# A two-layer vision tower: rotary partners by a shuffle, candidate lists merged by products, and a centring step without its own division

## The reference

```
h = tokens of 28x28 patches, class token, times a position table
h = layernorm(h + attention0(h))    # 8 heads of 16, rotary q and k, heads mixed before and after softmax
h = layernorm(h + ffn0(h))          # 16 experts; each takes its top 8 tokens of every image, results scatter-added
h = layernorm(h + attention1(h))    # causal attention blended with a moving average
h = layernorm(h + ffn1(h))          # 8 Sinkhorn rounds on 4160x8 gates; each expert takes its top 8 tokens of all
```

## Time and profile before

| | |
|---|---|
| time, median of 3 runs | 761.0 us (759.26 to 763.16) |
| the profiled execution | 762.83 us, span 761.0 us |
| granted TensorE clock, mean | 0.894 |
| PE busy | 587.0 us (77%) |
| DVE busy | 488.3 us (64%) |
| ACT busy | 336.0 us (44%) |
| POOL busy | 247.3 us (32%) |

### The profile page before, as it was taken

The page is one execution under the profiler, slowest core; times in us unless marked ns, Lnnn a source line. Parts: engine busy times, 40 slices in busy tenths (PEclk is TensorE's granted clock), DMA queues, the critical chain, the costliest instruction groups (busy, mean ns, idle before and its releaser), DMA issues. The chain is left out here.

```text
span 761.0 us, 20823 instructions
## 1 busy us (share of the span) xinstructions
PE 587.0 (77%) x8519; PEld 485.0 (64%) x8519; DVE 488.3 (64%) x880; ACT 336.0 (44%) x871; POOL 247.3 (32%) x251
## 2 busy tenths in 40 slices
PE   1999999999999999776179887766799999960002
PEld 1788888888888888664074476656677777740002
DVE  3175665666666666654536489955688888827852
ACT  0022444443444444453145356530578788846500
POOL 5344333333333333300104024432345555420001
PEclk9999999999999999987589999968699999965555
DMA  9364322222333379100430392000000000002200
GB/s 369 147 219 162 124 102 107 90 109 109 127 127 127 127 185 147 23 3 1 157 73 1 43 132 50 2 1 2 2 3 1 0 0 1 4 1 72 68 1 4
DMA packets 36813, 57.51 MB, mean 76 GB/s; under 512 B 20360, under 2 KB 33784, under 8 KB 34200
## 3 DMA queue, kind: packets, MB, share of 16 engines
q1 hardware_dynamic: 36666, 56.72, 26.4%
q0 software_dynamic: 96, 0.07, 0.0%
HBM read 50.24 MB, written 6.55 MB: 75 GB/s over the span
## 5 line engine op out<-in xcount | busy, mean ns | idle before, releaser
L387 PE MATMUL a_bank<-a_x,a_tok_w 128*128 128x256 f32 (+1 forms) x608 | 150.5, 390 | 16.0 <-DVE a_ht L640 16.0
L387 PEld LDWEIGHTS a_bank<-a_x,a_tok_w 128*128 128x128 f32 (+1 forms) x608 | 113.1, 192 | 37.6 <-issue 21.3
L129 POOL TENSOR_TENSOR a_qt<-a_qp,data 128x512 f32<-128x512 f32 x64 | 71.9, 1153 | 2.1 <-POOL a_qp L751 1.6
L751 POOL TENSOR_TENSOR a_qp<-a_rope 128x260 f32<-128x260 f32 x16 | 11.7, 734 | 168.9 <-DVE a_rope L575 168.9
L287 ACT ACTIVATE a_at<-a_bank 65x256 f32<-65x256 f32 x128 | 38.9, 390 | 25.0 <-PE a_bank L264 25.0
L569 DVE SCALAR_TENSOR_TENSOR a_ht<-a_bank,data 128x256 f32<-128x256 f32 x16 | 7.7, 484 | 64.6 <-PE a_bank L387 64.6
L1182 POOL TENSOR_TENSOR base<-h_tok,bias 65x512 f32<-65x512 f32 x16 | 29.8, 1866 | 55.2 <-ACT h_tok L1165 55.2
L1562 POOL TENSOR_TENSOR b_e<-b_e,b_inv 128x585 f32<-128x585 f32 (+1 forms) x32 | 35.4, 1109 | 23.7 <-DVE b_inv L1412 23.7
L264 PE MATMUL a_bank<-a_mix,a_e 64*65 64x64 f32 x1024 | 38.6, 227 | 2.2 <-ACT a_at L287 2.2
L200 ACT ACTIVATE a_e<-a_e 128x390 f32<-128x390 f32 (+1 forms) x48 | 24.1, 510 | 32.1 <-DVE a_e L180 32.0
L264 PEld LDWEIGHTS a_bank<-a_mix,a_e 64*65 64x65 f32 x1024 | 34.2, 140 | 6.0 <-issue 3.9
(11 more groups left out here) (255 smaller groups left out, 1452.5 us busy)
## 6 DMA issues: line engine op xcount, KB each, us to landing
a_x<-in_x SPq DMA_DIRECT2D x16, 2304.0 KB, 7.8
lag_rows<-a_kernel SPq DMA_DIRECT2D x1, 4192.5 KB, 38.3
lags<-lag_rows SPq DMA_DIRECT2D x1, 2112.5 KB
out<-e_plain SPq DMA_DIRECT2D x16, 130.0 KB
expert_weights<-in_w SPq DMA_DIRECT2D x2, 1024.0 KB, 6.0
lags<-lag_rows SPq DMA_DIRECT2D x1, 2047.5 KB
base<-places SPq DMA_DIRECT2D x1, 1560.0 KB
a_tok_w<-in_tok_w SPq DMA_DIRECT2D x1, 1152.0 KB, 6.8
```

What stands on the lines that cost most here:

```text
L129: nc.gpsimd.tensor_tensor(qt[:, b * BLOCKS * P:(b + 1) * BLOCKS * P].rearrange("p (c h i) -> p c h i", i=qb, h=HEADS), wide(by_image[:, b, ...
L387: mm = nc.tensor.matmul(banks[0][:, 0:GP], w[0:rows, k * DIM:(k + 1) * DIM], x[p][0:rows, k * GP:(k + 1) * GP], start=(k == 0), stop=(k == ...
```

## The change

It has three parts.

1. Rotary in `embed_and_attend`. The products with `wqs` and `wks` and their tables go. One query and one key product follow each other, into banks 6 and 7, and keys no longer wait for the rotated queries. DVE multiplies each by the cosine and by the sine table (whose rows are now swapped), and one `stream_shuffle` of the query's and the key's sine halves (128x520) swaps partitions i and i^4. `EMBED` moves fillers. `scale` now stands ahead of `normalise` in DVE's loop.
2. `scatter_and_norm`: the multiplication by 1/128 goes; the subtraction becomes one `scalar_tensor_tensor` that takes the sums with the factor -1/128 and adds.
3. `norm_and_route`: the four DRAM writes and reads of the lists and the chosen tokens go. The lists are spread by a masked product on DVE (`by_list`), then by a matrix product with a 0/1 table into 64 rows of 128; the choice is made on 64 partitions; the 64x64 table comes from a product with ones. Three small tables are added to the input, four 128-column weight blocks and two columns are removed.

```diff
-EMBED = (0, 4, 5, 11, 15, KT + 1)
+EMBED = (0, 3, 6, 11, 15, KT + 1)
...
                 wait_past(pe, S.tok_saved, g - 3)
-                product(6, D("wq"), h)
-                product(7, D("wqs"), h).then_inc(S.q_done, 1)
-
-            def keys(g, h):
-
-                pe.wait_ge(S.rope_a, 2 * g + 2)
-                product(6, D("wk"), h)
-                product(7, D("wks"), h).then_inc(S.k_done, 1)
+                product(6, D("wq"), h).then_inc(S.q_done, 1)
+                product(7, D("wk"), h).then_inc(S.k_done, 1)
...
-                rotate(0, 6, "bq", cos4, S.rope_a)
-                rotate(1, 7, "bqs", sin4, S.rope_a)
+                rotate(sine[:, 0, :], 6, "bq", sin4).then_inc(S.rope_ka, 1)
+                rotate(cosine[:, 0, :], 6, "bq", cos4).then_inc(S.rope_a, 1)
 
             def rotate_keys(g):
                 dve.wait_ge(S.k_done, g + 1)
-                rotate(2, 6, "bk", cos4, S.rope_ka)
-                rotate(3, 7, "bks", sin4, S.rope_ka)
-                dve.wait_ge(S.rope_ka, 2 * g + 2)
-                nc.vector.tensor_tensor(kt[:, :].rearrange("p (b t) -> p b t", b=GI), rope[2][:, :, :],
-                                        rope[3][:, :, :], ALU.add).then_inc(S.kt_ready, 1)
+                rotate(sine[:, 1, :], 7, "bk", sin4).then_inc(S.rope_ka, 1)
+                dve.wait_ge(S.rope_ka, 3 * g + 2)
+                rotate(cosine[:, 1, :], 7, "bk", cos4).then_inc(S.rope_ka, 1)
+                nc.vector.stream_shuffle(swapped[:, :, :], sine[:, :, :], [i ^ 4 for i in range(32)]).then_inc(S.rope_swapped, 1)
+                dve.wait_ge(S.rope_ka, 3 * g + 3)
+                dve.wait_ge(S.rope_swapped, g + 1)
+                nc.vector.tensor_tensor(kt[:, :], cosine[:, 1, :], swapped[:, 1, :], ALU.add).then_inc(S.kt_ready, 1)
...
                     values(g + 1, 1 - p)
+                if exists(g - 1):
+                    scale(g - 1)
+                if exists(g + 1):
                     normalise(nc, dve, g + 1, e[1 - p], total, inv, S)
                 if exists(g - 1):
-                    scale(g - 1)
                     save_logits(g - 1)
...
-                pool.wait_ge(S.rope_a, 2 * g + 2)
-                nc.gpsimd.tensor_tensor(qp[:, :].rearrange("p (b t) -> p b t", b=GI), rope[0][:, :, :],
-                                        rope[1][:, :, :], ALU.add).then_inc(S.q_sum, 1)
+                pool.wait_ge(S.rope_a, g + 1)
+                pool.wait_ge(S.rope_swapped, g + 1)
+                nc.gpsimd.tensor_tensor(qp[:, :], cosine[:, 0, :], swapped[:, 0, :], ALU.add).then_inc(S.q_sum, 1)
...
                 nc.vector.tensor_reduce(total[n % 3][:, :], summed, AX.X, ALU.add).then_inc(S.summed, 1)
                 dve.wait_ge(S.summed, n + 1)
-                nc.vector.tensor_scalar(mean[n % 3][:, :], total[n % 3][:, :], 1.0 / DIM, None,
-                                        ALU.mult).then_inc(S.mean_ready, 1)
-                dve.wait_ge(S.mean_ready, n + 1)
...
-                nc.vector.tensor_tensor(zc[n % 3][:, :, :], summed, wide(mean[n % 3][:, :].unsqueeze(2), [TOKENS, GI, DIM]),
-                                        ALU.subtract).then_inc(S.centred, 1)
+                nc.vector.scalar_tensor_tensor(out=zc[n % 3][:, :, :], in0=wide(total[n % 3][:, :].unsqueeze(2), [TOKENS, GI, DIM]),
+                                               scalar=-1.0 / DIM, in1=summed, op0=ALU.mult, op1=ALU.add).then_inc(S.centred, 1)
...
+            def in_lists(n, a):
+                nc.vector.tensor_tensor(by_list[:, n, :, :], wide(T("list_of").unsqueeze(2), [P, LISTS, TOP]),
+                                        wide(a[:, :].unsqueeze(1), [P, LISTS, TOP]), ALU.mult).then_inc(S.listing, 1)
...
             then(nc.vector.max(best[:, :], cand[:, :]))
+            in_lists(0, best)
             then(nc.vector.max_index(place[:, :], best[:, :], cand[:, :]))
             then(nc.vector.tensor_copy(placef[:, :], place[:, :]))
-            nc.vector.tensor_scalar(placef[:, :], placef[:, :], T("block_base"), None, ALU.add).then_inc(S.listed, 1)
-
-            dve.wait_ge(S.lists, 32)
-            then(nc.vector.max(top[:, :], lv[:, :]))
-            then(nc.vector.max_index(pos[:, :], top[:, :], lv[:, :]))
+            then(nc.vector.tensor_scalar(placef[:, :], placef[:, :], T("block_base"), None, ALU.add))
+            in_lists(1, placef)
+
+            dve.wait_ge(S.lists, 1)
+            then(nc.vector.tensor_copy(lists[:, :], banks[2][0:SL, 0:P]))
+            then(nc.vector.max(top[:, :], lists[:, :]))
+            then(nc.vector.max_index(pos[:, :], top[:, :], lists[:, :]))
             then(nc.vector.tensor_copy(posf[:, :], pos[:, :]))
-            then(nc.vector.tensor_tensor(hit[:, :, :], wide(T("iota", E).unsqueeze(1), [E, TOP, P]),
-                                         wide(posf[:, :].unsqueeze(2), [E, TOP, P]), ALU.is_equal))
-            then(nc.vector.tensor_tensor(hit[:, :, :], hit[:, :, :], wide(ln[:, :].unsqueeze(1), [E, TOP, P]), ALU.mult))
-            nc.vector.tensor_reduce(chosen[:, 0, :], hit[:, :, :], AX.X, ALU.add).then_inc(S.chosen, 1)
-            nc.vector.tensor_scalar(chosen[:, 1, :], top[:, :], 0.5, None, ALU.is_gt).then_inc(S.chosen, 1)
-
-            dve.wait_ge(S.slots, 48)
+            then(nc.vector.tensor_tensor(posf[:, :], posf[:, :], T("slot_of", SL), ALU.mult))
+            then(nc.vector.tensor_reduce(at[:, :], posf[:, :], AX.X, ALU.add))
+            dve.wait_ge(S.lists, 2)
+            then(nc.vector.scalar_tensor_tensor(out=hit[:, :], in0=T("iota", SL), scalar=at[:, :], in1=banks[3][0:SL, 0:P],
+                                                op0=ALU.is_equal, op1=ALU.mult))
+            then(nc.vector.tensor_reduce(mine[:, 0:1], hit[:, :], AX.X, ALU.add))
             nc.vector.tensor_copy(take[:, :], mine[:, 0:1]).then_inc(S.index, 1)
-            then(nc.vector.tensor_scalar(same[:, :], everyone[:, :], mine[:, 0:1], None, ALU.is_equal))
+            nc.vector.tensor_scalar(alone[:, :], T("ident", SL)[:, 0:SL], mine[:, 0:1], None, ALU.mult).then_inc(S.chosen, 1)
...
+            dve.wait_ge(S.everyone, 1)
+            then(nc.vector.tensor_scalar(same[:, :], banks[4][0:SL, 0:SL], mine[:, 0:1], None, ALU.is_equal))
...
+            for n in range(2):
+                pe.wait_ge(S.listing, n + 1)
+                nc.tensor.matmul(banks[2 + n][0:SL, 0:P], T("slots_of_expert"),
+                                 by_list[:, n, :, :].rearrange("p l k -> p (l k)"), start=True, stop=True).then_inc(S.lists, 1)
+            pe.wait_ge(S.chosen, 1)
+            nc.tensor.matmul(banks[4][0:SL, 0:SL], T("ones", SL)[:, 0:SL], alone[:, :], start=True,
+                             stop=True).then_inc(S.everyone, 1)
```

More of the change, by code:

```diff
@@ L326, in embed_and_attend @@
         ht = [sb(f"ht{i}", [P, GI, TOKENS]) for i in range(2)]
-        rope = [sb(f"rope{i}", [P, GI, TOKENS]) for i in range(4)]
+        cosine, sine, swapped = (sb(n, [P, 2, GT]) for n in ("cosine", "sine", "swapped"))
         qp, kt = sb("qp", [P, GT]), sb("kt", [P, GT])
@@ L828, in route_and_gather @@
         banks = [ctx.enter_context(nc.psum_tensor(f"r_bank{i}", [P, 512], F32)) for i in range(8)]
-        S = named_semaphores(R.ctx, nc, "r_", "step shifted exp_done probs turned best saved loaded loaded_rest read ident_done "
+        S = named_semaphores(R.ctx, nc, "r_", "step shifted exp_done probs turned best saved loaded loaded_rest read "
                   "picked gathered stored adapt bv_spread value_bias padded")
@@ L1044, in scatter_and_norm @@
         zc = [sb(f"zc{i}", [TOKENS, GI, DIM]) for i in range(3)]
[L1045 to L1046 removed]
+        total, var, sd, rs = ([sb(f"{n}{i}", [TOKENS, GI]) for i in range(3)]
+                                          for n in ("total", "var", "sd", "rs"))
         T = lambda name, rows=P: R.tables[0:rows, TABLES[name][0]:TABLES[name][0] + TABLES[name][1]]
@@ L1598, in norm_and_route @@
         banks = [ctx.enter_context(nc.psum_tensor(f"e_bank{i}", [P, 512], F32)) for i in range(6)]
-        S = named_semaphores(R.ctx, nc, "e_", "step col_sum col_done turned listed saved lists chosen chosen_saved slots index "
+        S = named_semaphores(R.ctx, nc, "e_", "step col_sum col_done turned listed listing lists chosen everyone index "
                   "got turned2 x_ready y_done y_ready turned3 gated mixed squared root scattered weights "
```

68 lines of the change are left out of this document (25 added, 43 removed).

## The result

| | before | after |
|---|---|---|
| time, median of 4 runs each | 761.11 us (759.26 to 763.16) | 718.26 us (717.28 to 718.97) |
| ratio, 95% interval | | 0.9435 (0.9408 to 0.9463) |
| span of the profiled execution | 761.0 us | 716.8 us |
| granted TensorE clock, mean | 0.894 | 0.900 |

A forecast was written before the change was run, and what follows sets the result against it. PE's order bounds `embed_and_attend`, DVE `scatter_and_norm`, and one chain of DVE steps and DMA round trips the final selection. Gains of 19.6 + 12.9 + 10.2 = 42.7 us take 761.0 to 718 us; 8 in 10 between 712 and 727.

The forecast's parts named there:

- 0.88 + 0.53: `embed_and_attend`, per period: two products fewer on PE save 0.88 us, the vanished wait for `a_hw` ahead of the tail 0.53.
- 18.6 us named as a sign: `embed_and_attend`: a period of 18.6 us would show the forecast right.
- forecast 11.9 to 13.0: `embed_and_attend`: with scores at 108.78, `a_hw` ends by 120.7, or by 121.8 if held up by a whole POOL piece.
- 15 x 0.88: `embed_and_attend`: removed products save 0.88 us in 15 of 16 groups, 13.2 us; the last iteration with keys counts nothing.
- 19.6 us: `embed_and_attend`: whole gain of part 1, 13.2 us from products and 6.4 from the wait in 12 periods.
- PE's clock: Rival: where the clock rises and falls between stages may shift, 3 us either way; larger loss or several shortfalls, chance 0.04.
- Forecast 12.9: `scatter_and_norm`: eleven intervals shrink from 4.20 to 3.2 us, 11.0, plus 1.9 in the drain; ends 9.6 and 14.2.
- a long loop: `scatter_and_norm`: loop from scatter over sums, subtraction and ACT to the scatter two groups on, 6.15 us for two intervals.
- Forecast 10.2: `norm_and_route`: best candidates to `e_take` falls from 14.4 to 4.2 us, products hidden; fetch still ends last, 0.5 us cover.
- The wait for `a_hw`: Rival in `embed_and_attend`: PE still waits 0.5 us every period, 6.4 us less gain, 724.5 us; chance 0.11.
- The new centring: Rival in `scatter_and_norm`: it waits for POOL as the multiplication did, part 2 gives next to nothing, 731 us; chance 0.06.
- The 1.9: Slower rival, `embed_and_attend`: shuffle time above 1.9 us is waiting in 12 to 13 periods; 5.2 eats all; chance 0.02.

The follow-up runs named there:

- part1: The kernel before with the rotary part alone (with `EMBED` and DVE's new order): 746.36 us, ratio 0.9797.
- part3: The kernel before with only the lists merged by products in `norm_and_route`: 751.25 us, ratio 0.9863.
- part2: The kernel before with the new centring of `scatter_and_norm` alone: 747.62 us, ratio 0.9805.
- sums_in_psum: The kernel before with the sums in PSUM instead of SBUF, the multiplication by 1/128 kept: 749.59 us, ratio 0.9821.
- after_again: The changed kernel itself, unaltered, run once more beside other kernels: 718.74 us, ratio 0.9425.
- order_back: The changed kernel with `scale` put back behind `normalise` in DVE's loop: 734.88 us, ratio 0.9637.
- shuffle_x2: The changed kernel with one more shuffle of the same size, result unused, ahead of the real one: 717.20 us, ratio 0.9406.
- shuffle_x4: The changed kernel with three more shuffles of the same size, results unused, ahead of the real one: 737.69 us, ratio 0.9668.

## Why the prediction was right, and where it was off

**Part 1, period.** Forecast 0.88 + 0.53 = 1.41 less per period, measured 1.35; 12 periods give 16.2 of 16.9 us. What is missing is in the wait, 0.45 and not 0.53. (The 18.6 us named as a sign belong to the shorter of two alternating periods, 20.02 before and 18.70 after; the longer one went from 20.5 to 19.2.) The mechanism held at every step: shuffle 0.73, `a_hw` slowed by POOL but in time, wait gone. Its end lies 115.83 - 104.24 = 11.6 us behind the scores, forecast 11.9 to 13.0: I let both `a_kt` and `a_hw` pay for POOL, and only `a_hw` did. The Trainium skill (SBUF — State Buffer, "Who interferes with whom") makes two such instructions exclude each other whenever they overlap; `a_hw` bears that out with 903 in the median for 430, and `a_kt` with 429 once it no longer overlaps.

**Part 1, the ends: the step that failed.** "15 x 0.88" counted three groups outside the twelve at 0.88 each, 2.6 us. The groups ahead gave 2.3 together in the first profile (77.20 to 74.91), 1.7 in *part1* (75.52). The last period, which has no fillers left, gave nothing: 13.94 us before, 13.89 in *part1*. So by *part1*'s profile the stage gains 17.8 of 19.6 us: 0.8 are missing in the periods, 0.9 at the two ends, 0.1 behind the last `a_vs`. In the first profile of the kernel after, the last period is 16.54 us, 2.6 longer than before, and this makes the 15.7.

These 2.6 us are the clock at 0.50 between 304 and 313, and *part1* has the same code with 13.89. The code of before has both, too: the last period is 13.9 in *before* and *part3*, 16.3 in *part2*, and 13.0 in *sums_in_psum*. The same place in *before*, then in *sums_in_psum* (columns as above):

```profile
323.00:327.00 4.00, 3.58 (x96) 3.25 (x96) 2.18 (x3) 1.22 (x4) 0.73 (x2) 0.57 0.02 4
```

```profile
319.00:323.00 4.00, 1.37 (x34) 1.22 (x34) 3.93 (x5) 1.62 (x6) 4.00 (x5) 1.00 0.00 0
323.00:327.00 4.00, 2.86 (x105) 2.56 (x105) 2.49 (x3) 1.88 (x7) 1.03 (x2) 1.00 0.02 4
```

In *sums_in_psum* PE is busy 1.37 of 4 us, and the clock does not fall at all in the next four. The low stretch differs between executions, then, and what sets its length stays open; so does whether the new code has the long one more often (two profiles of three, against one of four). This is the rival "PE's clock", in a place that I had not named, and within the 3 us given to it.

**Part 2, mis-sized.** Forecast 12.9, measured 16.2. The interval is 3.10, not 3.2, which is the 3.08 of the rows without POOL; I had leaned towards a long loop worked out from sums of waits. Eleven intervals at 1.10 and the last 1.9 are 14.0. All fifteen intervals are at 3.1 now, with 0.6 more in the fourth, which already met POOL (3.69): 14.6. The last 1.6 is the clock at the stage's start, 0.74 and 0.83 in the first two stretches of 4 us before, 1.00 after. It is no gain of this part: *part1* and *part3*, with the old centring, show 1.00 there too. The stage ahead is 1.6 us longer in them, so that routing, experts and scattering together are 144.0 us before, 144.1 in *part1* and *part3*, 129.4 in *part2*, 129.0 after. The -1.2 of the stage ahead is of this kind: its clock is 0.68 and 0.90 between 374 and 382 after, and 1.00 in the same place of its code before. The two do not always go together: *sums_in_psum* has both the longer routing (70.9 us) and the low clock behind it.

**Part 3.** Forecast 10.2, measured 10.6: the steps to `e_take` took 3.7 us for 4.2, both products hid, the cover of the fetch is 1.9 and not 0.5 us.

**Moving average and attention1.** 2.9 us less was not forecast. The code is the same; *after_again* has 1.4 us more in `moving_average` and 0.9 more in attention1 than the first profile of the same kernel; in the first two stretches of 4 us of `moving_average` its clock is 0.50 and 0.76, where the other has 0.65 and 1.00. The code of these stages is the same in every kernel here, and all fourteen profiles lie between 177.5 and 180.5 us: a difference between executions, in `moving_average` of the clock, with the first profile of the kernel after at the lower end.

**The rivals.** The wait for `a_hw` did not stay, though *order_back* shows how near it was. The new centring does not wait for POOL; *sums_in_psum* shows for the old multiplication that a source in PSUM was enough for this. A shuffle would have become dear from 0.73 + 1.4 = 2.1 us on, an estimate, where I had put 1.9, but by way of `a_vs`; *shuffle_x2* and *shuffle_x4* show the start of the kernel paying before that. The 1.9 itself was a slip: it left out the piece of POOL's that the same text let `a_hw` lose (121.8 against 121.97 with a shuffle of 0.71), and with it would have been 0.9.

**Luck.** The errors of 3.9 and 3.3 us cancelled, and some 2.6 of the first and 1.6 of the second are the clock of single executions; 2.9 us more came from stages whose code did not change. The total is better than its parts deserve.

## What to carry to other kernels

Work taken from the engine that bounds a stage counts only as far as the engines that feed it keep ahead: 0.88 us less for PE per period were worth nothing until DVE's order let `a_hw` come 2.9 us earlier after the scores (14.5 to 11.6), so price such edits together and look up what each product will wait for in the new order. Before removing a small instruction that takes ten times its usual time, see what runs beside it: here, moving its operand to PSUM alone brought nearly all of the gain. At the ends of a pipelined loop, count neither full periods nor a steady clock; and before explaining 2 us at such a place by the kernel, look at a second profile of the same code.
